# Moving the end of the latent attention later, and sharing the gated sum between GpSimd and VectorE, in a two-layer transformer kernel

## The reference, cut to what matters

```
xn = layernorm(x);  s = retention(xn);         f = local_transformer(xn)   # 2 layers
x  = x + s * silu(f)                                                       # the "gated sum"
xn = layernorm(x);  s = latent_attention(xn);  f = mixture_of_experts(xn)
x  = x + s * silu(f)
```

## Time and profile before

| | |
|---|---|
| times of three runs | 3194.14, 3197.83, 3198.21 us; median 3197.83 |
| profiled execution | 3194.56 us, span 3192.8 us |
| PE, DVE, ACT, POOL busy in the span | 2830.2, 1594.8, 1182.2, 1067.1 us |
| stages 0 to 7 | 90 to 1189.8 us, some 138 us each |
| stage 8 | 1189.8 to 1337.0 us |
| stages 9 to 14 | 1337.0 to 2358.0 us, 165 to 174 us each |
| stages 15 and 16 | 2358.0 to about 2567 us |
| experts | about 2567 us to the end |

### The profile page before, as it was taken

One profiled execution on the slowest core, in us unless ns is written; L12 is line 12 of the kernel. 1 busy time (PEld: TensorE's weight loads), 2 busy tenths in 40 slices (PEclk: granted clock), 3 DMA queues, 4 the chain that ended last, 5 costly groups with the idle time before them and its releaser, 6 DMA issues. The chain is left out here.

```text
span 3192.8 us, 42318 instructions
## 1 busy us (share of the span) xinstructions
PE 2830.2 (89%) x15646; PEld 1892.9 (59%) x15646; DVE 1594.8 (50%) x3890; ACT 1182.2 (37%) x2240; POOL 1067.1 (33%) x769
## 2 busy tenths in 40 slices
PE   6999999999999998998989898989888669999990
PEld 4565655656566565555554545455544358889990
DVE  6656656565565646475757575656555410000002
ACT  4444453444435344343434444434432212222221
POOL 5424334232433424353535353525331301111112
PEclk8999999999999999899989998999978679999995
DMA  3000000000000011000000001010101069898875
GB/s 128 10 24 26 25 14 24 21 17 24 27 28 38 24 42 57 4 28 23 27 21 24 27 9 42 4 47 4 40 4 40 20 256 345 330 352 324 327 289 161
DMA packets 86055, 261.73 MB, mean 82 GB/s; under 512 B 10941, under 2 KB 50189, under 8 KB 67165
## 3 DMA queue, kind: packets, MB, share of 16 engines
q1 hardware_dynamic: 79372, 241.26, 20.8%
q0 software_dynamic: 6480, 17.77, 1.5%
HBM read 210.69 MB, written 44.12 MB: 80 GB/s over the span
## 5 line engine op out<-in xcount | busy, mean ns | idle before, releaser
L1168 POOL TENSOR_TENSOR s_qk<-s_qk,s_rrec 128x1024 f32<-128x1024 f32 (+1 forms) x128 | 215.2, 1681 | 719.8 <-DVE s_rrec L1321 719.7
L959 ACT ACTIVATE s_qk<-s_qk,s_mx 128x256 f32<-128x256 f32 (+1 forms) x512 | 239.9, 470 | 398.8 <-DVE s_mx L1315 398.8
L551 PE MATMUL s_pA<-s_w_wqkv,s_curT 128*128 128x512 f32 x768 | 367.8, 618 | 5.6 <-ACT s_curT L935 3.7
L1917 DVE COPY m_xT<-m_px 128x256 f32<-128x256 f32 x71 | 30.1, 424 | 479.1 <-PE m_px L1836 479.1
L1847 PEld LDWEIGHTS m_ph<-m_xT,m_w 128*128 128x128 f32 x2272 | 266.1, 193 | 5.4 <-issue 1.8
L1847 PE MATMUL m_ph<-m_xT,m_w 128*128 128x128 f32 x2272 | 266.7, 276 | 1.2 <-DVE m_xT L1917 1.2
L1861 PE MATMUL m_py<-m_w,m_hT 128*128 128x256 f32 x1136 | 258.5, 381 | 0.0
L694 PE MATMUL s_pD<-s_mixer 32*128 32x512 f32 (+3 forms) x1024 | 205.9, 521 | 53.7 <-DVE s_pairs L1410 38.5
L551 PEld LDWEIGHTS s_pA<-s_w_wqkv,s_curT 128*128 128x128 f32 x768 | 145.7, 197 | 179.4 <-issue 166.7
L1410 DVE TENSOR_SCALAR s_pairs<-s_pD 128x1024 f32<-128x1024 f32 (+1 forms) x192 | 193.8, 1038 | 103.9 <-PE s_pD L694 71.9
L1781 POOL DMA_INDIRECT acc_s<-m_y,m_goal x71 | 68.1, 959 | 482.3 <-ACT m_y L1880 482.3
(11 more groups left out here) (220 smaller groups left out, 5006.9 us busy)
## 6 DMA issues: line engine op xcount, KB each, us to landing
m_w<-in_m_w SPq DMA_DIRECT2D x142, 1024.0 KB, 5.6
m_xin<-rows_s SPq DMA_DIRECT2D x71, 129.0 KB
m_acc<-acc_s SPq DMA_DIRECT2D x16, 512.0 KB, 5.1
s_cur<-in_x SPq DMA_DIRECT2D x8, 512.0 KB, 3.4
xn_s<-s_cur SPq DMA_DIRECT2D x8, 512.0 KB, 2.6
s_s_tm<-xn_s SPq DMA_DIRECT2D x8, 512.0 KB, 3.2
cur_s<-s_cur SPq DMA_DIRECT2D x8, 512.0 KB, 2.6
s_s<-s_s_tm SPq DMA_DIRECT2D x8, 512.0 KB, 2.6
```

The source lines that it names most:

```text
L551: last = nc.tensor.matmul(out, lhs(c), rhs(c), start=(c == 0), stop=(c == n - 1))
L959: last = nc.scalar.activation(pi, pi, ACT.Exp, scale=-1.0, bias=mx[:, u, i:i + 1], accum_out=rsum[:, u, i:i + 1])
L1168: nc.gpsimd.tensor_tensor(pi, pi, rrec[:, u, :].unsqueeze(2).broadcast_to((P, 4, 256 - lo)), ALU.mult).then_inc(p_rdy, 1)
```

## The change: what it does

1. Late tail. Rounds 0 and 1 of pair 7's scores move from step t = 3 to after the t loop, round 2 into c = 0. `latent_exp(7)` on ACT moves from before the c loop to after `gelu(0)`. At t = 3, `v` comes before `av` 2. `av` 3 moves from c = 1 to c = 3, the ranks from c = 2 to c = 3, `aTM` 3 from c = 2 to c = 4 (so ranks now come before it), `attnT` from c = 3 to c = 5, and `lo` from u = 2, 3 to u = 3, 4; the second `lo` stands between `x1T` and the latent projections. The router's picks on DVE move behind `gate_up(0)`.
2. To make room, `attnT` lies in `curT` (the turned input of the stage) instead of `sq`, and `hT[3]`, `hT[4]` in `PT_even`, `hT[5]` elsewhere in `pairs`. ACT's wait before `attn_in` goes, and one before `stream_in` comes.
3. POOL's order in a u step. `ret_norms`, `reciprocal_roots` and `query_sum` come before `scale_probabilities`, and the root for the input norm comes at u = 6 instead of 7. This touches the retention stages too.
4. Gated sum. POOL does `s_tm * cur` (`stream_products`) and the sum with `x_tm` (`token_sums`), four each in a stage. DVE keeps the product with (1 + tanh), and the four statistics (`token_stats`) now come together at u = 2.

```diff
@@ PE, in the t loop and after it (ring lists and other engines alike)
-                    if s.behind:
+                    if s.behind and t < 3:
                         latent_scores(b - 1, 4 + t, (0, 1))
...
+                    if s.ahead:
+                        v_product(k + 1, t)
                     if s.behind and t == 3:
                         latent_values(b - 1, 2)
-                    if s.ahead:
-                        v_product(k + 1, t)
...
-                    if s.behind and t == 3:
-                        latent_scores(b - 1, 4 + t, (2,))
+                if s.behind:
+                    latent_scores(b - 1, PAIRS - 1, (0, 1))
@@ PE, in the c loop
+                    if s.behind and c == 0:
+                        latent_scores(b - 1, PAIRS - 1, (2,))
-                    if s.behind and c == 1:
+                    if s.behind and c == 3:
                         latent_values(b - 1, 3)
-                    if s.behind and c == 2:
+                    if s.behind and c == 3:
+                        ranks(b - 1)
+                    if s.behind and c == 4:
                         by_token(b - 1, 3)
-                        ranks(b - 1)
-                    if s.behind and c == 3:
+                    if s.behind and c == 5:
                         pe.wait_ge(outD, doneD["aTM", b - 1, 3])
@@ PE, in the u loop
-                    if s.behind and u in (2, 3):
-                        latent_output(b - 1, u - 2)
+                    if s.behind and u == 3:
+                        latent_output(b - 1, 0)
...
+                    if s.behind and u == 4:
+                        latent_output(b - 1, 1)
+                    if s.lat and u == 4:
                         latent_projections(b)
@@ ACT
-                if s.behind:
-                    latent_exp(b - 1, PAIRS - 1)
                 for c in range(NHC):
                     if s.here:
                         gelu(k, c)
...
+                    if s.behind and c == 0:
+                        latent_exp(b - 1, PAIRS - 1)
@@ POOL, new functions
+            def stream_products(b, i):
+                if i == 0:
+                    pool.wait_ge(xs_in, 32 * (b + 1))
+                pool.wait_ge(outD, doneD["w2", B + b, i])
+                for t in (2 * i, 2 * i + 1):
+                    nc.gpsimd.tensor_tensor(s_tm[:, t, :], s_tm[:, t, :], cur[b % 2][:, t, :], ALU.mult).then_inc(gated, 1)
+
+            def token_sums(b, i):
+                for t in (2 * i, 2 * i + 1):
+                    pool.wait_ge(gate_rdy, NT * b + t + 1)
+                    nc.gpsimd.tensor_tensor(x_tm[:, t, :], x_tm[:, t, :], z[:, t, :], ALU.add).then_inc(x1_rdy, 1)
@@ POOL, in the u loop
+                    if s.ret and u in (4, 6, 8):
+                        ret_norms(k, u // 2 - 2)
+                    if s.ret and k + 2 < B and u == 6:
+                        reciprocal_roots(var_1, rstd_1, k + 2)
+                    if s.lat and u == 1:
+                        stream_products(b, 0)
+                        token_sums(b, 0)
+                        stream_products(b, 1)
+                    if s.lat and u == 2:
+                        token_sums(b, 1)
+                        reciprocal_roots(var_x, rstd_x, b)
+                    if s.lat and u in (5, 6, 8):
+                        query_sum(b, (u - 4) // 2)
                     if s.ahead and u < 2 * NT:
                         scale_probabilities(k + 1, u)
-                    (the same calls, which stood behind it)
@@ DVE
             def gated_sum(b, t):
-                (wait for xs_in and w2; s_tm * cur)
                 dve.wait_ge(fin_silu, NT * b + t + 1)
                 dve.wait_ge(gated, NT * b + t + 1)
-                step(nc.vector.scalar_tensor_tensor(out=z[:, t, :], ... ))
-                nc.vector.tensor_tensor(x_tm[:, t, :], x_tm[:, t, :], z[:, t, :], ALU.add).then_inc(x1_rdy, 1)
+                nc.vector.scalar_tensor_tensor(out=z[:, t, :], ... ).then_inc(gate_rdy, 1)
+
+            def token_stats(b, t):
                 dve.wait_ge(x1_rdy, NT * b + t + 1)
                 ln_stats(t, [x_tm[:, t, :]])
```

More of the change, by code:

```diff
@@ L174, in ring_d_jobs @@
         if s.behind:
-            j += [("aTM", b - 1, 2)]
+            j += [("sc", b - 1, 7, 0), ("sc", b - 1, 7, 1), ("aTM", b - 1, 2)]
         for c in range(NHC):
@@ L195, in ring_d_jobs @@
                 j += [("rout", k, 0)]
-            if s.behind and u in (2, 3):
-                j += [("lo", b - 1, u - 2)]
+            if s.behind and u in (3, 4):
+                j += [("lo", b - 1, u - 3)]
             if s.lat and u == 4:
@@ L1589, in _ @@
                         rotary_parts(k + 1, t - 1)
-                    if s.behind and t == 3:
-                        clipped(b - 1, 4 + t, (0, 1))
                     if s.ret:
                         ret_rotary(k, t)
-                    if s.behind:
+                    if s.behind and t < 3:
                         clipped(b - 1, 4 + t, (2,))
@@ L1604, in _ @@
                 if s.behind:
+                    clipped(b - 1, PAIRS - 1, (0, 1))
                     by_token(b - 1, 2)
@@ L1620, in _ @@
                         gate_up(k, c)
+                    if s.behind and c == 0:
+                        clipped(b - 1, PAIRS - 1, (2,))
                     if s.ahead and c == 0:
                         scale_qk(k + 1, 3)
+                    if s.behind and c == 0:
+                        router_probabilities(b - 1)
+                        router_pick(b - 1, 0)
+                        router_pick(b - 1, 1)
+                        router_weights(b - 1)
                     if s.prep and c == 1:
                         again_stats(k + 1)
-                    if s.behind and c == 2:
-                        by_token(b - 1, 3)
+                    if s.behind and c == 3:
                         router_ranks(b - 1)
@@ L1629, in _ @@
                         row_ends(b - 1, 0)
+                    if s.behind and c == 4:
+                        by_token(b - 1, 3)
                     if s.prep and c == 4:
@@ L1671, in _ @@
                         ffn_out(k, 1)
-                    if s.behind and u in (2, 3):
-                        latent_out(b - 1, u - 2)
                     if s.lat and u == 2:
@@ L1676, in _ @@
                         gated_sum(b, 3)
+                        for t in range(NT):
+                            token_stats(b, t)
                         ln_variances(var_x)
@@ L1679, in _ @@
                         tokens_apply(b)
+                    if s.behind and u in (3, 4):
+                        latent_out(b - 1, u - 3)
                     if s.lat and u == 4:
```

51 lines of the change are left out of this document (19 added, 32 removed).

## The result

The changed kernel takes 3109.93 us (median of four runs, 3106.89 to 3110.90) against 3195.98 us before in the same comparison: ratio 0.973, 95% interval 0.9713 to 0.9747. The profiled execution takes 3110.9 us around a span of 3109.1, so 83.7 us less than the one of before. 3120 us was forecast, 74.5 us less.

A forecast was written before the change was run, and what follows sets the result against it. PE was taken to bound the kernel, with its waits and the low clock following them. Terms: -13 + 3 - 17.5 - 12 - 29 - 6 - 2 + 2 = -74.5, from 3194.56 to 3120 us; range 3080 to 3145.

The forecast's parts named there:

- Item 1: End of the t loop, stages 9 to 14: PE's 2.20 us wait for clipped scores goes, -13 us.
- 2, late tail: In the c loop: extra table loads stay hidden, attnT's copy ahead of the first local scores costs +3 us.
- item 5: Clock in stages 8 to 14: 75 us of low time goes, at 0.39 each, -29 us.
- Item 3: u = 1 to 4, stages 8 to 14: shared gated sum and GpSimd's order gain 2.5 us a stage, -17.5 us.
- rival C: Stages 8 to 14: GpSimd's sums bind the norm and the kernel gets slower, 3230 us; chance 0.07.
- rival B: Loads of x_tm and s_tm land over 1.5 us later than reckoned, delaying GpSimd's operations: 3148 us; chance 0.07.
- Item 4: Query sum ahead of the scaling on GpSimd: PE's 11.9 us of waits for the rotated query go, -12 us.
- I take 40%: Share of the low-clock time in stages 8 to 14 taken to go; the bounds were none or all, 0 and -73.
- Rival A: Stages 8 to 14: waits go, but new short waits at u = 2 to 4 keep the clock low: 3149 us; chance 0.17.
- Item 6: Retention stages: ret_norms(1) ahead of the scaling ends VectorE's 0.88 us wait, 8 x 0.8 = -6 us.
- Item 7: Ends: stage 15 gains in front of its up-projection, -2 us; the chain in stage 16 costs +2 us.
- some 3.5 us later: Stage 16: pair 7's scores come after av 2, their third round after by_token(2), a delay of some 3.5 us.

The follow-up runs named there:

- e3: The changed kernel with the whole gated sum back on VectorE, late tail and new GpSimd order kept: 3099.13 us, ratio 0.9688.
- e1: The kernel before with only GpSimd's new order in the u steps: 3132.25 us, ratio 0.9795.
- e2: The kernel before with only the query sum moved ahead of the scaling on GpSimd: 3148.60 us, ratio 0.9844.
- e4: The kernel before with GpSimd's new order and the shared gated sum, without the late tail and its memory: 3122.94 us, ratio 0.9770.
- e9: The changed kernel itself, unaltered, timed once more in five rounds: 3111.38 us.
- e10: The changed kernel with the gated sum wholly on VectorE, timed once more on one chip beside the change: 3100.69 us.

## Why the prediction was right, and where its terms were off

*Item 1, end of the t loop, and 2, late tail: -13 and +3 forecast, 0 found.* At equal low time A is as long with the late tail as before (82.7 us after and 82.5 to 82.9 before at 6.8 us of low time; 81.2 in e3 and before at 3.4). Its mean even rose by 1.0 us, since after has 6.8 us of low time in all six stages and before had 3.4 in four of them; that is counted under item 5. The step that failed is "`av` 2 now stands behind `v`, where its mask is just ready" and "what PE then needs from it, `gate_up(0)`, is wanted only by the third up-projection": the mask was 1.50 us late, and `aTM` 2 needs a bank of pair 7 that DVE has yet to clip, 2.64 us. The lower bound, 0, was the right end. Of the +3 us at `attnT` the trace shows 1.7, six waits of 0.3 for ACT's copy. The two table loads cost PE nothing: it waits for no GELU in A after, where before it waited 0.6 us for one in each stage.

```profile
2022.23 1.28 ACT L1034 ACT_TABLE_LOAD   x1
2023.52 2.34 ACT L1034 ACTIVATE s_pairs<-s_pairs 128x2560 f32<-128x2560 f32 x1
2025.88 1.28 ACT L1016 ACT_TABLE_LOAD   x1
```

Between load and neighbour stand 0.01 to 0.02 us. Stage 13 has four loads of 1.28 us after and two before, so the two more take 2.6 us of ACT's time, as forecast.

*Item 3, sharing and order: -17.5 forecast, -16.5 found* (piece B: 2.1 us in each of stages 9 to 14 and 3.8 in stage 8). In stages 9 to 14 1.2 us of the 2.1 come from the order (e1 against e2) and 0.7 to 0.9 from the sharing (after against e3, e4 against e1); the prediction put the 2.5 us down to both together and had no split. Two of its signs did not come: the latent projections start 2.2 us earlier behind `w2` and not 4, after a wait of 1.08 us and not below 1. GpSimd's price was taken right, and rival C falls with it; rival B falls because GpSimd never waits for the loads of the streams.

*Item 4, query sum: -12 forecast.* The wait is gone, 11.9 us.

*Item 5, clock: -29 forecast, about -42 found.* Low time of stages 8 to 14 fell from 195 to 92 us, by 102 and not the 75 forecast. 14 us of the 102 lie in B, where they are worth nothing; the other 88, at 0.43 to 0.47 each, are 38 to 41 us. What stages 8 to 14 gained besides items 3 and 4 is about the same: 70.3 - 16.5 - 11.9 = 41.9. The step that was too small is "I take 40%", and the price, 0.39, a little. The 2 in the forecast's low time holds, since the low level in the records is 0.50. The forecast did not say which wait weighed most. e2 says it: the 1.71 us ahead of the latent scores carried most of it, more than 7 us in D of stage 13. Rival A, that the new short waits keep the clock low as the long ones did, falls: in C the low time went from 34 us to none.

*Item 6, retention: -6 forecast, -4.7 found*, 1.0 us in most stages (137.8 to 136.9). e2, without that part of the order, keeps stages of 137.8 us, and e1 has the 136.9, which gives it to `ret_norms` and the input norm's root together; no run parts the two.

*Item 7, ends: 0 forecast, -9.4 found.* The step "some 3.5 us later" counted the third round's way behind `av` 2 and not that `av` 2 itself stood behind two rounds of scores; and the clock was counted for stages 8 to 14 alone. e4 has the old order, and there PE shows in stage 16

```profile
2445.97 3.78 PE L695 MATMUL s_pD<-s_mixer 32*128 32x512 f32 x12 [0.41 <-DVE s_pairs L1425]
2449.69 3.47 PE L705 MATMUL s_pA<-s_pairs,s_mixer 128*32 128x512 f32 x32
2461.32 4.47 PE L705 MATMUL s_pA<-s_pairs,s_mixer 128*32 128x512 f32 x32 [4.49 <-POOL s_pairs L1182]
```

and after

```profile
2435.63 3.59 PE L710 MATMUL s_pA<-s_pairs,s_mixer 128*32 128x512 f32 x32 [0.17 <-POOL s_pairs L1193]
2449.52 4.49 PE L710 MATMUL s_pA<-s_pairs,s_mixer 128*32 128x512 f32 x32 [5.92 <-POOL s_pairs L1193]
```

From `av` 2 to `av` 3 it is 2.3 us more (13.9 for 11.6), from `av` 1 (2405.74 after, 2415.56 in e4) to `av` 2 it is 4.2 less: 2.0 us in all, some of it again the clock. Of the other 7 us 5.8 lie ahead of `av` 1 and go with the clock (low time there 43 us for 56 in e4, of both stages 91 for 110). It isn't steady: e9, the same kernel, has 203.2 us there with 98 us low.

The sum lands near because items 1 and 2 gave 10 less than forecast, and the clock and the ends 22 more. The direction and most mechanisms were right; that the total was within 10 us owes something to errors of opposite sign.

*What stays open.* In e3 the wait of 2.64 us stands in every stage from 9 to 14, and in four of them, stages 10 to 13, A has 3.4 us of low time or none; after, it has 6.8 in all six. So the same wait is or is not followed by low clock. Even one kernel differs between executions: stage 9 has 17.1 us of low time in e3 and 6.8 in e10. That the kernel without the sharing is 11 us faster than the change is measured, twice; that it is the low clock is read from A, 1.7 to 1.9 us shorter on average, while B is 0.7 longer and D within 0.4. Why the sharing, which itself only shortens B by 0.7 us, brings the low stretch back in A of the next stage was not found. Also untested is the collision at the end of the t loop: no run keeps the change's order and parts the two products of GpSimd and VectorE.

## What to carry to other kernels

Look for the wait behind which the engine's clock is low for long, not for the longest wait: 1.7 us, for an instruction queued behind one that wasn't ready, cost some 45 us over seven stages (e2), of which 12 were the wait and the rest went with the low clock. A wait that is taken away can move to the next user of the same bank, as here 2.20 us turned up there as 2.64; follow the list of ring jobs to that one, and the reader's own order on the other engine, before counting the gain. When a part of a change looks harmful, test it again beside another fix: the sharing cost 11 us beside one order of the clips and gained 9 beside the other.

## What the hardware showed that was not expected

- A DVE product with two SBUF operands (`scale_qk`) that started 0.06 us behind a GpSimd product took 3.37 us instead of 1.21, once in each of the stages 9 to 14: in stage 13 it ends 1.08 us after GpSimd's product; the norm of four tiles took 3.21 us instead of 1.67 beside a scaling of 1.89 us (GpSimd from 2065.69). These two GpSimd instructions took their usual times (medians 2.35 and 1.89); the mask that followed the first, issued while DVE's product ran, took 1.71 us instead of 0.73. So here GpSimd's work beside VectorE's cost time on VectorE, 2.16 and 1.54 us by these rows, and not only on GpSimd, 0.98 us. What made the instructions longer, the rows do not show.
- PE doing 16 useless transposes in a wait of 2.64 us made a kernel of 3110 us 14 us faster (median; its four times spread over 18 us).
- Six stages of the same work can settle on one length (160.4 to 160.6 us after) or not (156.8 to 163.3 in e3) with the same wait of 2.64 us at the end of the t loop.
